# Distance attention: row normalisation, projections, norms and the first unit's stacks in one block

## The chip, the cores and the metric

The kernel runs on one core of a Trainium2 chip. Five engines work side by side: TensorE (PE; its weight loads are PEld), VectorE (DVE), ScalarE (ACT), GpSimd (POOL) and SyncE (SP), which here only issues DMAs. Each runs its own instructions in order, and they wait for one another on semaphores. The metric is the device time of one execution in microseconds, lower is better. The kernel before took 3648.4 us in the median of 3 runs (3647.82 to 3649.07).

## The reference

A "macaron" of six layers over `x` of 4 x 1024 x 128 in float32: a gelu feed-forward, a distance attention, the same feed-forward, two local-attention layers, a causal attention, and the two local layers again. Only the distance attention is changed. Its reference, where the input is the layer-normalised `x` and the result is added to `x`:

```python
Q = (x @ W_k.T).reshape(B, S, H, dk).transpose(0, 2, 1, 3)      # B=4, S=1024, H=16, dk=8
sq_norm = jnp.sum(Q * Q, axis=-1, keepdims=True)
dot = jnp.einsum('bhsk,bhtk->bhst', Q, Q)
scores = -(sq_norm - 2.0 * dot + sq_norm.transpose(0, 1, 3, 2)) * inv_sqrt_dk
attn = jax.nn.softmax(scores, axis=-1)
context_q = jnp.einsum('bhst,bhtk->bhsk', attn, Q)
merged = jnp.einsum('hkd,hvd->hkv', Wq_h, Wv_h)
attn_out = jnp.einsum('bhsk,hkv->bhsv', context_q, merged) * inv_sqrt_dk
return attn_out.transpose(0, 2, 1, 3).reshape(B, S, D) @ W_o.T
```

## The kernel before

The kernel is a sequence of blocks (`nc.Block()`). All engines meet at the end of a block, and `clear()` behind it is one more meeting of all engines that resets the semaphores. The stages of `distance_attention` are such blocks, in this order. `P` is 128, `NT` 32 tiles of 128 rows, `TPB` 8 tiles per batch.

1. A block in which SyncE issues the loads of the weights (L297 to L301).
2. `normalised_columns` (called in L302). It begins with `row_statistics`, one block (a table load and a square root on ScalarE, a reciprocal on VectorE). Then comes a block of eight steps of four tiles: VectorE normalises four rows of `xn` (`normalise`, L90, from SBUF to SBUF), TensorE transposes them into PSUM (L1319), ScalarE copies them to `xT` (L1330). `xn` has two buffers.
3. The projection block (L303 to L393). GpSimd sets `v`, `query` and `keys` with ten memsets of 128x1024 and then two small ones (L307 to L313). For each of 4 batches TensorE makes `q` in rows (L335, eight products, to slot 0) and in columns (L342, two products, to slot 1), and, one batch late, the squared norms (L327, to slot 2). ScalarE copies `q_all` (L361), then the high part `q_hi` (L364, rounded to float32r) and the squares `sq` (L367), then the high part of the norms `n_hl` (L356). VectorE subtracts to get the low parts: `q_lo` (L391) and the low half of `n_hl` (L384). All these VectorE operations have PSUM as a source. `merged` and `w_eff` are two 128x128 products of weights at the start.
4. The attention loop. A unit is one batch and four heads; there are 16. For each unit SyncE issues 40 DMAs from SBUF to SBUF (`stack`, L435 to L439) that lay the high and low parts of `q` and the norms one under the other in `query[k]` and `keys[k]`, k being 0 for even and 1 for odd units: 4 heads x 8 DMAs of 8 rows by 1024, and 2 of norms. The stack of unit u waits until unit u - 2 has made all its scores; those of units 0 and 1 wait for nothing. TensorE waits for the unit's 40 DMAs, then makes 32 jobs of scores (L466), ScalarE takes the exponential of each (L530, 128x1024), TensorE multiplies it with `v` (L481). Units 0 to 3 and 12 to 15 are written out; 4 to 11 are a hardware loop of two turns.
5. A block for the output product and the sum with `X` (L571, L578, L595).

What orders the work is only the order of the instructions on each engine and the semaphores.

Of the kernel before, what the change touches and what calls it, by code (L numbers as in the profile page):

```python
# [229 lines left out]
def distance_attention(nc, c, wk_d, wv_d, wo_d, sel_d):  # L230
# [17 lines left out]
    with ExitStack() as st:  # L248
# [16 lines left out]

        with ExitStack() as st2:
            sem, clear = semaphores(nc, st2, first=150)
            loaded = sem("loaded")
            q_ready = sem("q_ready")
# [14 lines left out]
            def sb2(name, shape, dt=F32):  # L284
                return st2.enter_context(nc.sbuf_tensor(c.fresh(name), shape, dt))
            xT = sb2("xT", [P, NT * P])
            wv = sb2("wv", [P, P])
# [14 lines left out]
            normalised_columns(nc, c, xT, moments=False)  # L302
            with nc.Block() as block:  # L303
                @block.gpsimd
                def _(pool):
                    for k in range(2):
                        pool.memset(v[k][:], 0.0).then_inc(cleared, 1)  # L307
                        for p in range(2):
                            pool.memset(query[k][p][:].bitcast(F32), 1.0).then_inc(cleared, 1)
                            pool.memset(keys[k][p][:].bitcast(F32), 1.0).then_inc(cleared, 1)  # L310
                    pool.wait_ge(cleared, 10)
# [4 lines left out]
                def _(pe):  # L316
                    pe.wait_ge(loaded, 80)
                    pe.matmul(c.slots[2][:, 0, 0:P], wv[:], wk[:], start=True, stop=True).then_inc(cross_ready, 1)

                    def norms(b):  # L320

                        pe.wait_ge(sq_ready, b + 1)
                        if b:
                            pe.wait_ge(norm_hi_ready, b)
                            pe.wait_ge(norm_lo_ready, b)
                        for half in range(2):
# [3 lines left out]

                    for b in range(B):
                        if b:
                            pe.wait_ge(q_out, b)
                        for t in range(TPB):
                            m = pe.matmul(c.slots[0][:, t // 4, (t % 4) * P:(t % 4 + 1) * P],  # L335
                                          xT[:, (b * TPB + t) * P:(b * TPB + t + 1) * P], wk[:], start=True, stop=True)
                        m.then_inc(q_ready, 1)
# [7 lines left out]
                        if b == 0:  # L345
                            pe.wait_ge(merged_ready, 1)
                            pe.matmul(c.slots[3][:, 0, 0:P], merged[:], wo[:], start=True, stop=True).then_inc(eff_ready, 1)
                        if b:
                            norms(b - 1)
                    norms(B - 1)  # L350

                @block.scalar
                def _(act):
                    def norm_out(b):
                        act.wait_ge(norm_ready, b + 1)
                        act.activation(n_hl[0:HEADS, b * S:(b + 1) * S], c.slots[2][0:HEADS].rearrange(flat),  # L356
                                       ACT.Copy).then_inc(norm_hi_ready, 1)

                    for b in range(B):
                        act.wait_ge(q_ready, b + 1)  # L360
                        act.activation(q_all[:, b * TPB:(b + 1) * TPB, :, :].rearrange("p t h d -> p (t h d)"),  # L361
# [6 lines left out]
                        if b:  # L368
                            norm_out(b - 1)
# [1558 lines left out]
```

## Time and profile before

| | |
|---|---|
| runs, median of 3 | 3648.4 us (3647.82 to 3649.07) |
| profiled execution | 3644.16 us |
| its span in the trace | 3642.4 us |
| TensorE's mean granted clock | 0.965 |
| PE busy | 3169.9 us, 87% of the span |
| VectorE busy | 2107.0 us, 58% |
| ScalarE busy | 2088.0 us, 57% |
| GpSimd busy | 1727.0 us, 47% |

The table is a mean over six layers with different limits. The page's list of 40 slices of the span shows the distance attention as the first long stretch without VectorE (its digit is 0 in slices 3 to 7, of 91 us each) and with TensorE at 9; ahead of it the second slice has TensorE at 5 only. For a single stage one reads the timeline and the waits of its own stretch; the times there count from the start of the span.

### The profile page before, as it was taken

The page shows a single profiled execution, that of the slowest core. Times are in us where ns is not written, and L with a number is a line of the kernel's source. Part 1 is how long each engine was busy: PE and PEld are TensorE (multiplying, and loading weights), DVE is VectorE, ACT ScalarE, POOL GpSimd, SP SyncE. Part 2 cuts the span into 40 slices and gives each one's busy share as a digit, 9 for nine tenths or more (in the row PEclk, how much of TensorE's full clock was granted, in tenths as well). Part 3 has the DMA queues.
Part 4 walks back from the last instruction along what each step waited for, and adds up shares of the span by engine and source line. Part 5 has one row for each costly group of instructions (what it writes and reads, how often), then busy time and mean ns, then how long its engine had stood idle before and what let it go on. Part 6 is the DMA issues. An engine that isn't in the chain of part 4 may idle for free. (4 is left out here: it accounts for less than half of the span.)

```text
span 3642.4 us, 72895 instructions
## 1 busy us (share of the span) xinstructions
PE 3169.9 (87%) x26438; PEld 1944.9 (53%) x26564; DVE 2107.0 (58%) x4204; ACT 2088.0 (57%) x3388; POOL 1727.0 (47%) x1348
## 2 busy tenths in 40 slices
PE   6599999858889988749999999999996688999885
PEld 4222222535566656526666666666664455666663
DVE  4200000458887777555555555555555688777773
ACT  2499999425555555435555555555553455555552
POOL 1100000058888888513333333333332788888882
PEclk9799999979999999979999999999998899999998
DMA  1122221021111111000000000000000211111111
GB/s 33 21 38 39 36 39 30 7 81 34 33 34 34 35 35 34 22 10 9 6 9 6 9 6 9 6 9 6 7 7 29 63 36 33 35 36 36 35 32 32
DMA packets 124405, 95.70 MB, mean 26 GB/s; under 512 B 80448, under 2 KB 100544, under 8 KB 123968
## 3 DMA queue, kind: packets, MB, share of 16 engines
q1 hardware_dynamic: 122784, 89.41, 11.2%
q10 hardware_dynamic: 1440, 3.80, 0.3%
q8 instruction: 122, 2.00, 0.2%
q14 instruction: 59, 0.48, 0.0%
HBM read 22.90 MB, written 2.10 MB: 7 GB/s over the span
## 5 line engine op out<-in xcount | busy, mean ns | idle before, releaser
L1737 POOL TENSOR_SCALAR e<-e,inv 128x768 f32<-128x768 f32 (+7 forms) x512 | 375.1, 745 | 763.6 <-DVE inv L1629 763.6
L1700 ACT ACTIVATE e<-e,nmax 128x768 f32<-128x768 f32 (+7 forms) x512 | 395.4, 772 | 429.6 <-DVE e L1624 427.1
L1624 DVE TENSOR_SCALAR_CACHE_REDUCE e<-slot 128x768 f32<-128x768 f32 (+7 forms) x512 | 376.5, 754 | 242.6 <-PE slot L1513 242.6
L530 ACT ACTIVATE e<-slot 128x1024 f32<-128x1024 f32 x512 | 472.5, 1087 | 38.0 <-PE slot L466 38.0
L880 POOL TENSOR_TENSOR inv_norm<-floored,minus_half 128x16 f32<-128x16 f32 x128 | 374.1, 2923 | 10.7
L1617 DVE COPY eT<-slot 128x512 f32<-128x512 f32 (+3 forms) x384 | 239.0, 622 | 235.4 <-PE slot L1524 235.3
L1117 ACT ACTIVATE probT<-slot 128x1024 f32<-128x1024 f32 x128 | 131.1, 1024 | 376.4 <-PE slot L973 376.4
L1524 PE MATMUL slot<-ident,e 128*128 128x128 f32 x2304 | 332.9, 280 | 8.4 <-DVE eT L1617 3.5
L852 POOL TENSOR_TENSOR prob<-prob,inv_total 128x1024 f32<-128x1024 f32 x128 | 242.7, 1896 | 200.4 <-DVE inv_total L1209 200.4
L1507 PE MATMUL slot<-key,q 64*128 64x512 f32 (+3 forms) x1536 | 318.1, 518 | 19.2 <-ACT v L1687 12.8
L873 POOL TENSOR_TENSOR rot<-cosine,sine 128x1024 f32<-128x1024 f32 x128 | 301.9, 2359 | 53.3 <-DVE sine L1191 53.2
L1524 PEld LDWEIGHTS slot<-ident,e 128*128 128x128 f32 x2304 | 253.2, 141 | 92.4 <-issue 69.4
L929 PE MATMUL slot<-w_qk,hT 128*128 128x512 f32 x512 | 259.2, 629 | 30.3 <-DMA b<-in_local_b_dram 18.7
L481 PE MATMUL slot<-e,v 128*32 128x512 f32 x2048 | 277.0, 614 | 0.4 <-ACT e L530 0.4
L1539 PE MATMUL slot<-eT,v 128*64 128x256 f32 x2048 | 254.6, 385 | 0.9 <-DVE X L1640 0.9
L466 PE MATMUL slot<-query,keys 36*128 36x512 f32 x1024 | 209.5, 474 | 45.3 <-DMA keys<-n_hl 31.8
L845 POOL TENSOR_TENSOR rot<-rot,inv_norm 128x1024 f32<-128x1024 f32 x128 | 243.5, 1902 | 0.3
L541 DVE COPY oT<-slot 128x512 f32<-128x512 f32 x32 | 22.1, 692 | 366.1 <-PE slot L481 366.1
L466 PEld LDWEIGHTS slot<-query,keys 36*128 36x128 f32 x1024 | 87.7, 187 | 267.9 <-ACT e L530 217.6
L449 POOL COPY v<-q_all 128x256 f32<-128x256 f32 (+1 forms) x16 | 6.4, 401 | 472.3 <-PE slot L481 449.8
L1094 ACT ACTIVATE sq<-slot 128x1024 f32<-128x1024 f32 x128 | 131.2, 1025 | 148.7 <-PE slot L929 148.7
L988 PE MATMUL slot<-probT,v_mix 128*64 128x64 f32 x2048 | 132.7, 228 | 88.5 <-ACT probT L1117 88.5
(158 smaller groups left out, 6443.7 us busy)
## 6 DMA issues: line engine op xcount, KB each, us to landing
v_mix<-v SPq DMA_DIRECT2D x256, 128.0 KB, 2.3
w_qkv<-in_causal_w_dram SPq DMA_DIRECT2D x32, 192.0 KB
query<-q_hi SPq DMA_DIRECT2D x128, 32.0 KB
keys<-q_hi SPq DMA_DIRECT2D x128, 32.0 KB
query<-q_lo SPq DMA_DIRECT2D x128, 32.0 KB
keys<-q_lo SPq DMA_DIRECT2D x128, 32.0 KB
hs<-H SPq DMA_DIRECT2D x32, 128.0 KB
h1s<-H SPq DMA_DIRECT2D x32, 128.0 KB
```

The source lines that it names most:

```text
L466: m = pe.matmul(out[:, h, :], keys[k][p][rows, t * P:(t + 1) * P], query[k][p][rows, half * 512:half * 512 + 512], start=True, stop=True)
L481: m = pe.matmul(c.slots[3][32 * j:32 * j + 32, half, :], v[k][:, t, j, :], e[(n - 1 + j // 2) % E_RING][:, j % 2 * 512:j % 2 * 512 + 512], ...
L530: act.activation(e[n % E_RING][:], c.slots[n % RING][:].rearrange(flat), ACT.Exp, scale=2 * SCALE).then_inc(e_ready, 1)
L873: pool.tensor_tensor(rot[:, a.j, :, :].rearrange(flat), cosine[:], sine[:], ALU.add).then_inc(rot_ready, 1)
L880: pool.tensor_tensor(inv_norm[:], floored[:], minus_half[:].broadcast_to([P, 2 * HEADS]), ALU.pow)\
L929: m = pe.matmul(bank_qk[:, half, :], hT[:, a.j * P:(a.j + 1) * P], w_qk[a.depth][:, half * 512:half * 512 + 512], start=True, stop=True)
L1507: pe.matmul(c.slots[h][:, bank, 0:hi - lo], q[k][rows, i * P:(i + 1) * P], key[k][rows, lo:hi], start=True, stop=True)
L1524: m = pe.transpose(turn[:, bank, t * P:(t + 1) * P], e[n % RING][h][:, (at + t) * P:(at + t + 1) * P], c.ident[:])
L1539: m = pe.matmul(o[64 * h:64 * h + 64, place(one) // 4, place(one) % 4 * P:(place(one) % 4 + 2) * P], v[k][:, t, 64 * h:64 * h + 64], eT[pa ...
L1624: dve.tensor_scalar(e[n % RING][h][:, 0:cols], c.slots[h][:].rearrange(flat)[:, 0:cols], -1.0, None, ALU.mult, ALU.min, accum_out=nmax[:, ...
L1700: act.activation(part, part, ACT.Exp, bias=nmax[:, n, h:h + 1], scale=-1.0, accum_out=total[:, n, h:h + 1]).then_inc(e_ready, 1)
L1737: pool.tensor_scalar(part, part, inv[:, n, h:h + 1], 1.0, ALU.mult, ALU.mult).then_inc(scaled, 1)
```

## The change

The normalisation of rows, their transposition, the projections and the norms become one block, and the DMAs of unit 0 are issued in it.

- Only `row_statistics` stays a block of its own. The rest of `normalised_columns` moves into the projection block; one block and one `clear()` go. The transposes now go to slot 3, and the small product for `w_eff` to slot 2.
- Per batch: TensorE makes columns, the transposes of the next batch's two groups, rows, norms. ScalarE: `q_hi`, `sq`, two copies of transposed columns, high norms, `q_all`. VectorE: eight rows of the next batch, `q_lo`, low norms. The norms are no longer one batch late.
- SyncE has a part in this block. It waits for five memsets and `q_hi` of batch 0, issues the 16 DMAs of the high parts, waits for `q_lo`, issues 16, waits for both parts of the norms, issues 8. GpSimd's memsets are reordered so that the buffers of even units and `v[0]` are the first five.
- In the loop, unit 0 has no stack left; unit 1 and the others keep theirs, with the same number of DMAs in another order within a head.
- The two `stacked` semaphores are made outside and cleared at the very end (`clear_stacked()`), one more meeting of all engines.

The functions `high`, `low` and `norms` of `stack_head` issue 4, 4 and 2 DMAs of a head. The diff, shortened:

```diff
+        def stack_head(sp, stacked, b, g, j):
+            k, cols = g % 2, bass.ds(b * S, S)
...
+            def high():
+                hi = q_hi[D * head:D * head + D, cols].bitcast(F32)
+                for at, dst in ((0, q_to), (0, k_to), (2, q_to), (1, k_to)):
+                    sp.dma_start(dst[to + at * D:to + at * D + D, :].bitcast(F32), hi).then_inc(stacked[k], 16)
+
+            def low():
+                lo = q_lo[D * head:D * head + D, cols].bitcast(F32)
+                for at, dst in ((1, q_to), (2, k_to), (3, q_to), (3, k_to)):
+                    sp.dma_start(dst[to + at * D:to + at * D + D, :].bitcast(F32), lo).then_inc(stacked[k], 16)
+
+            def norms():
+                both = n_hl[head:head + 33:32, cols].bitcast(F32)
+                sp.dma_start(q_to[to + 32:to + 34, :].bitcast(F32), both).then_inc(stacked[k], 16)
+                sp.dma_start(k_to[to + 34:to + 36, :].bitcast(F32), both).then_inc(stacked[k], 16)
+            return high, low, norms
+
+        stack_sem, clear_stacked = semaphores(nc, st, first=190)
+        stacked = [stack_sem("stacked_even"), stack_sem("stacked_odd")]
...
-            normalised_columns(nc, c, xT, moments=False)
+            row_statistics(nc, c, moments=False)
             with nc.Block() as block:
+                @block.sync
+                def _(sp):
+                    heads = [stack_head(sp, stacked, 0, 0, j) for j in range(GROUP)]
+                    sp.wait_ge(cleared, 5)
+                    sp.wait_ge(hi_ready, 1)
+                    for high, _, _ in heads:
+                        high()
+                    sp.wait_ge(lo_ready, 1)
+                    for _, low, _ in heads:
+                        low()
+                    sp.wait_ge(norm_hi_ready, 1)
+                    sp.wait_ge(norm_lo_ready, 1)
+                    for _, _, norms in heads:
+                        norms()
+
                 @block.gpsimd
                 def _(pool):
                     for k in range(2):
-                        pool.memset(v[k][:], 0.0).then_inc(cleared, 1)
                         for p in range(2):
                             pool.memset(query[k][p][:].bitcast(F32), 1.0).then_inc(cleared, 1)
                             pool.memset(keys[k][p][:].bitcast(F32), 1.0).then_inc(cleared, 1)
+                        pool.memset(v[k][:], 0.0).then_inc(cleared, 1)
                     pool.wait_ge(cleared, 10)
                     for k in range(2):
                         pool.memset(v[k][:, :, :, D:D + 1], 1.0).then_inc(cleared, 1)
 
...
+                    def turn_rows(i):
+                        pe.wait_ge(xn_ready, G * (i + 1))
+                        if i >= 2:
+                            pe.wait_ge(columns_ready, i - 1)
+                        for j in range(G):
+                            m = pe.transpose(c.slots[3][:, i % 2, j * P:(j + 1) * P], xn[:, i % 2, j, :], c.ident[:])
+                        m.then_inc(turned, 1)
+
+                    def columns(b):
+                        pe.wait_ge(columns_ready, 2 * b + 2)
                         if b:
                             pe.wait_ge(sq_ready, b)
                             pe.wait_ge(lo_ready, b)
...
+                    def rows(b):
+                        if b:
+                            pe.wait_ge(q_out, b)
...
+
+                    def norms(b):
+
+                        pe.wait_ge(sq_ready, b + 1)
+                        if b:
+                            pe.wait_ge(norm_hi_ready, b)
+                            pe.wait_ge(norm_lo_ready, b)
+                        else:
                             pe.wait_ge(merged_ready, 1)
-                            pe.matmul(c.slots[3][:, 0, 0:P], merged[:], wo[:], start=True, stop=True).then_inc(eff_ready, 1)
-                        if b:
-                            norms(b - 1)
-                    norms(B - 1)
+                            pe.wait_ge(eff_out, 1)
...
+                    pe.wait_ge(loaded, 80)
+                    pe.matmul(c.slots[2][:, 0, 0:P], wv[:], wk[:], start=True, stop=True).then_inc(cross_ready, 1)
+                    turn_rows(0)
+                    turn_rows(1)
+                    pe.wait_ge(merged_ready, 1)
+                    pe.matmul(c.slots[2][:, 1, 0:P], merged[:], wo[:], start=True, stop=True).then_inc(eff_ready, 1)
+                    for b in range(B):
+                        columns(b)
+                        if b < B - 1:
+                            turn_rows(2 * b + 2)
+                            turn_rows(2 * b + 3)
+                        rows(b)
+                        norms(b)
...
+                    def columns(i):
+                        act.wait_ge(turned, i + 1)
+                        act.activation(xT[:, i * G * P:(i + 1) * G * P], c.slots[3][:, i % 2, :], ACT.Copy).then_inc(columns_ready, 1)
+
+                    columns(0)
+                    columns(1)
                     for b in range(B):
...
                         act.wait_ge(qT_ready, b + 1)
                         act.activation(q_hi[:, b * S:(b + 1) * S], c.slots[1][:].rearrange(flat), ACT.Copy).then_inc(hi_ready, 1)
                         if b >= 2:
                             act.wait_ge(norm_ready, b - 1)
                         act.activation(sq[b % 2][:], c.slots[1][:].rearrange(flat), ACT.Square).then_inc(sq_ready, 1)
-                        if b:
-                            norm_out(b - 1)
-                    norm_out(B - 1)
+                        if b < B - 1:
+                            columns(2 * b + 2)
+                            columns(2 * b + 3)
+                        act.wait_ge(norm_ready, b + 1)
+                        act.activation(n_hl[0:HEADS, b * S:(b + 1) * S], c.slots[2][0:HEADS].rearrange(flat),
+                                       ACT.Copy).then_inc(norm_hi_ready, 1)
+                        act.wait_ge(q_ready, b + 1)
+                        act.activation(q_all[:, b * TPB:(b + 1) * TPB, :, :].rearrange("p t h d -> p (t h d)"),
+                                       c.slots[0][:].rearrange(flat), ACT.Copy).then_inc(q_out, 1)
...
                 def _(dve):
+                    def rows(i):
+                        if i >= 2:
+                            dve.wait_ge(turned, i - 1)
+                        for j in range(G):
+                            normalise(dve, c, i * G + j, xn[:, i % 2, j, :]).then_inc(xn_ready, 1)
+
+                    rows(0)
+                    rows(1)
                     dve.wait_ge(cross_ready, 1)
                     dve.wait_ge(loaded, 80)
                     dve.scalar_tensor_tensor(merged[:], c.slots[2][:, 0, 0:P], SCALE, block_mask[:], ALU.mult, ALU.mult)\
                        .then_inc(merged_ready, 1)
                     dve.wait_ge(eff_ready, 1)
-                    dve.tensor_copy(wo_eff[:], c.slots[3][:, 0, 0:P]).then_inc(eff_out, 1)
-
...
                     for b in range(B):
                         cols = slice(b * S, (b + 1) * S)
+                        if b < B - 1:
+                            rows(2 * b + 2)
+                            rows(2 * b + 3)
                         dve.wait_ge(hi_ready, b + 1)
                         dve.wait_ge(sq_ready, b + 1)
                         dve.tensor_tensor(q_lo[:, cols], c.slots[1][:].rearrange(flat), q_hi[:, cols].bitcast(F32),
                                           ALU.subtract).then_inc(lo_ready, 1)
-                        if b:
-                            norm_low(b - 1)
-                    norm_low(B - 1)
+                        dve.wait_ge(norm_hi_ready, b + 1)
+                        dve.tensor_tensor(n_hl[32:32 + HEADS, cols], c.slots[2][0:HEADS].rearrange(flat),
+                                          n_hl[0:HEADS, cols].bitcast(F32), ALU.subtract).then_inc(norm_lo_ready, 1)
             clear()
...
                     def stack(b, g, first=False, last=False):
-                        k, cols = g % 2, bass.ds(b * S, S)
-                        if not first and not (isinstance(b, int) and b == 0 and g == 1):
+                        if first:
+                            return
+                        if not (isinstance(b, int) and b == 0 and g == 1):
                             sp.wait_ge(s_ready, JOBS * (GROUPS * b + g - 1))
...
+                            for part in stack_head(sp, stacked, b, g, j):
+                                part()
...
             clear()
+        clear_stacked()
```

## Rows read from the trace of the kernel before

**Rows 1.** Waits from 160 to 660 us (total, times, longest).
```profile
ACT e L530 <- PE slot L466: 38.0, 22, 28.3
...
PE slot L466 <- DMA keys<-n_hl: 31.8, 1, 31.8
```

**Rows 2.** Timeline from 137 us: start, duration, engine, line; idle time in brackets.
```profile
137.85 0.89 SPq L435 DMA_DIRECT2D query<-q_hi  x1
137.86 1.28 ACT L524 ACT_TABLE_LOAD   x1 [2.00 <-PEq L38]
...
164.77 0.51 SPq L439 DMA_DIRECT2D keys<-n_hl  x1
...
166.58 1.65 PE L466 MATMUL slot<-query,keys 36*128 36x512 f32 x6 [31.78 <-DMA keys<-n_hl]
...
167.42 5.61 ACT L530 ACTIVATE e<-slot 128x1024 f32<-128x1024 f32 x6 [28.28 <-PE slot L466]
```

**Rows 3.** Timeline, the normalised columns.
```profile
95.25 2.14 DVE L90 TENSOR_SCALAR xn<-X,moments,rstd 128x128 f32<-128x128 f32 x8 [0.73 <-PEq L38]
...
96.42 2.14 PE L1319 MATMUL slot<-ident,xn 128*128 128x128 f32 x8 [10.80 <-DVE xn L90]
...
97.57 0.60 ACT L1330 ACTIVATE xT<-slot 128x512 f32<-128x512 f32 x1 [3.44 <-PE slot L1319]
```

**Rows 4.** Timeline, the projection block.
```profile
106.12 0.95 POOL L307 MEMSET v<- 128x1024 f32 x1 [25.68 <-SPq L303]
...
108.24 1.88 PE L342 MATMUL slot<-xT,wk 128*128 128x512 f32 x4
...
110.16 1.02 ACT L364 ACTIVATE q_hi<-slot 128x1024 fp32r<-128x1024 f32 x1 [0.69 <-PE slot L342]
...
115.16 0.21 POOL L313 MEMSET v<- 128x32 f32 x2
...
120.98 1.89 PE L327 MATMUL slot<-sq,sel 128*16 128x512 f32 x4
...
131.27 3.53 PE L327 MATMUL slot<-sq,sel 128*16 128x512 f32 x4 [2.87 <-DVE n_hl L384]
...
135.88 1.21 DVE L384 TENSOR_TENSOR n_hl<-slot,n_hl 16x1024 fp32r<-16x1024 f32 x1 [4.76 <-ACT n_hl L356]
```

**Rows 5.** Timeline of SyncE's issues, stack of unit 2 and first issue of unit 3.
```profile
196.28 0.68 SPq L435 DMA_DIRECT2D query<-q_hi  x1
...
223.16 0.51 SPq L439 DMA_DIRECT2D keys<-n_hl  x1
...
225.96 0.68 SPq L435 DMA_DIRECT2D query<-q_hi  x1
```

**Rows 6.** Timeline of short windows, VectorE's rows beside GpSimd (local layers).
```profile
747.99 1.21 DVE L1174 TENSOR_SCALAR H<-X,moments,rstd 128x128 f32<-128x128 f32 x1 [1.10 <-PEq L38]
...
748.35 0.30 POOL L900 MEMSET kT<- 128x256 f32 x1
...
748.60 0.51 POOL L901 MEMSET v_mix<- 64x512 f32 x1
...
906.14 1.90 POOL L852 TENSOR_TENSOR prob<-prob,inv_total 128x1024 f32<-128x1024 f32 x1 [2.56 <-DVE inv_total L1209]
906.17 1.95 DVE L1174 TENSOR_SCALAR H<-X,moments,rstd  x1 [0.20 <-issue]
...
2807.62 1.59 DVE L1174 TENSOR_SCALAR H<-X,moments,rstd 128x128 f32<-128x128 f32 x1 [0.73 <-PEq L38]
```

**Rows 7.** Windows: stretch, length, busy PE, PEld, DVE, ACT, POOL, PE clock, DMA.
```profile
96.00:100.00 4.00, 3.40 (x13) 2.39 (x14) 3.63 (x15) 1.30 (x3) 0.00 (x0) 0.50 0.00 0
...
100.50:105.00 4.50, 2.90 (x18) 1.69 (x16) 3.60 (x15) 2.54 (x5) 0.00 (x0) 1.00 0.00 0
...
128.00:131.00 3.00, 0.40 (x1) 0.00 (x0) 2.32 (x2) 1.45 (x2) 0.00 (x0) 1.00 0.00 0
...
408.00:417.00 9.00, 9.00 (x40) 2.10 (x36) 0.69 (x1) 5.82 (x6) 0.40 (x1) 0.50 0.29 44
```

More of the change, by code:

```diff
@@ L263, in distance_attention @@
         ctx_all = sb("ctx_all", [P, NT, P])
+        def stack_head(sp, stacked, b, g, j):
+            k, cols = g % 2, bass.ds(b * S, S)
+            head = GROUP * g + j
+            to, q_to, k_to = 64 * (j % 2), query[k][j // 2], keys[k][j // 2]
+            def high():
[13 more added lines that the diff above has]
+        stacked = [stack_sem("stacked_even"), stack_sem("stacked_odd")]
         with ExitStack() as st2:
@@ L316, in _ @@
                 def _(pe):
[L317 to L322, printed above, removed]
-                        if b:
-                            pe.wait_ge(norm_hi_ready, b)
-                            pe.wait_ge(norm_lo_ready, b)
-                        for half in range(2):
-                            m = pe.matmul(c.slots[2][0:HEADS, half, :], sel[:], sq[b % 2][:, half * 512:half * 512 + 512],
-                                          start=True, stop=True)
-                        m.then_inc(norm_ready, 1)
-                    for b in range(B):
-                        if b:
[L333 to L337, printed above, removed]
+                    def turn_rows(i):
[7 more added lines that the diff above has]
+                        pe.wait_ge(columns_ready, 2 * b + 2)
                         if b:
@@ L344, in _ @@
                         m.then_inc(qT_ready, 1)
-                        if b == 0:
-                            pe.wait_ge(merged_ready, 1)
-                            pe.matmul(c.slots[3][:, 0, 0:P], merged[:], wo[:], start=True, stop=True).then_inc(eff_ready, 1)
-                        if b:
-                            norms(b - 1)
-                    norms(B - 1)
+                    def rows(b):
+                        if b:
+                            pe.wait_ge(q_out, b)
+                        for t in range(TPB):
+                            m = pe.matmul(c.slots[0][:, t // 4, (t % 4) * P:(t % 4 + 1) * P],
+                                          xT[:, (b * TPB + t) * P:(b * TPB + t + 1) * P], wk[:], start=True, stop=True)
+                        m.then_inc(q_ready, 1)
@@ new lines, in norms @@
+                    def norms(b):
[4 more added lines that the diff above has]
+                        else:
+                            pe.wait_ge(merged_ready, 1)
+                            pe.wait_ge(eff_out, 1)
+                        for half in range(2):
+                            m = pe.matmul(c.slots[2][0:HEADS, half, :], sel[:], sq[b % 2][:, half * 512:half * 512 + 512],
+                                          start=True, stop=True)
+                        m.then_inc(norm_ready, 1)
```

32 lines of the change are left out of this document (7 added, 25 removed).

## Prediction

> **What bounds the kernel now.** I read the list of waits first, between the start and the end of the attention loop. It shows one long wait of TensorE there, 31.8 us for a DMA into `keys`, once; ScalarE's exponentials waited 28.3 us for the same reason [rows 1]. Inside the loop ScalarE runs one exponential of 128x1024 after the other and nothing else ends late. So the loop itself is not touched by this change, and what can be won lies before its first score. The timeline of that stretch has three parts. The stacks: SyncE issues the 40 DMAs of unit 0 from 137.85 to 165.28, one after the other, and the first score matmul starts at 166.58, 1.3 us after the last issue [rows 2]. Before them, the normalised columns: VectorE's rows start at 95.25 and pass through TensorE and ScalarE [rows 3], until the next block opens at 106.1. Between the two, the projections: from 106.1 on; the last norm ends at 137.09, and the next block starts 0.76 us later [rows 2, 4]. Every stage waits for the end of the one before it, so 95.25 to 166.58, 71.3 us, is one chain. The question is how long it is when the three lie in one block.
>
> **The stacks.** All 40 DMAs are still issued, in another order (16 of the high parts, 16 low, 8 norms), so their issue takes the same 27.4 us [rows 2]. They now start when `hi_ready` of batch 0 and five memsets are there. They leave the path as long as the projections last longer than 27.4 us from that point on; below that is so by 2.5 us, and if that cover is lost SyncE ends the block and each microsecond counts in full. Queued behind SyncE's three waits is nothing but these DMAs. Unit 1's stacks move too: before, they were issued straight behind unit 0's, a little before the first score; now they start with the new loop block, with the first score. That is the position that all later units have: 40 issues from 196.28 to 223.67, plus the 1.3 us to land, against 29.68 us from one unit to the next [rows 5]. That fits with about 1 us to spare; I take nothing for it, between 0 and 1 us of loss.
>
> **The first batch of the merged block.** Let R be the start of VectorE's first row. Eight rows take 2.14 us [rows 3]; 0.1 to TensorE; the second four transposes at the low clock 1.1 (eight in 2.14) [rows 3]; the copy with its two hand-overs 0.8 (0.60 of it the copy) [rows 3]. Then `columns(0)`, four passes of 128x512, 1.88 at the full clock [rows 4]; the same count of passes at the low clock took 3.53 [rows 4]; as the clock rises in this stretch I take 2.7. Then the next two groups of transposes 1.1, `rows(0)` 1.95 (eight products, estimated from the 1.9 of its neighbours) [rows 4], `norms(0)` 1.89 [rows 4]. Norms of batch 0 are out at R + 11.8.
>
> **The period of the batches.** The old block needed 5.5 us a batch. The new one is slower, because VectorE now has the rows of the next batch queued behind `norm_low`: norms out of TensorE; high part on ScalarE 1.0, low part on VectorE 1.21 [rows 4], two groups of rows 2.14 [rows 3], one group of transposes 0.55 after the last, `rows` 1.95, `norms` 1.89, hand-overs 0.2: 8.95 us. Meanwhile TensorE has only `columns` to do, so it idles about 1.7 us in each. Two such periods are 17.9 us. The last batch has no rows: ScalarE is busy 2.0 us with the high norms and `q_all` of batch 2, then copy and square to 3.95, norms to 6.0, their two halves to 8.25. From R to the last low norm: 11.8 + 17.9 + 8.25 = 37.95 us.
>
> **What the change puts beside VectorE's rows.** The ten GpSimd memsets of `v`, `query` and `keys` stood in the projection block, where VectorE read PSUM. Now they start with the rows. They are back to back: 0.95 us each, and 9.04 us from the first to the two small ones behind them [rows 4]. What a row of this very form does beside GpSimd is in the trace: a row of 128x128, 0.26 us when alone, began at 747.99 in the middle of a string of memsets and took 1.21, ending when the 0.51 us memset of `v_mix` ended; the boundaries of several shorter memsets passed without it. The same in the second layer stage: 2807.62, until after the same memset [rows 6]. Beside a single tensor_tensor of GpSimd the row lasted 1.95 us, until that one ended, and passed before the next [rows 6]. GpSimd's first instruction comes out of a barrier about as early as VectorE's (both within 0.2 us), so one row may slip ahead, not eight. The cost of the ten memsets is thus bounded by 0 (no blocking) and 9.0 us (the rows wait for the whole string). I take 9.0, as the nearest rows are strings of memsets, and several boundaries passed there without the row. The Trainium skill (SBUF — State Buffer, "Who interferes with whom") says that VectorE in its two-port mode and GpSimd share a port pair as an exclusive lock, and that the later one blocks until the earlier instruction finishes. By that rule one row would pass at every boundary; rows 6 agree for tensor_tensor and differ for the short memsets. That result is the first rival below.
>
> **The sum.** R is 95.25 now and 95.2 + 9.0 = 104.2 after. Last low norm 104.2 + 37.95 = 142.15; block change 0.76 as now; first score 143.0 instead of 166.58: 23.6 us earlier. Off that go 0.35, since the exponential table load of 1.28 us, now hidden under the stacks [rows 2], starts with the first score, which needs 0.84 to the first exponential; and 0.4 for the extra barrier of `clear_stacked` (between 0 and the 0.76 of a whole block change). GpSimd's first `v` copy (first used five jobs later) costs nothing. Net 22.8 us. `hi_ready` comes at about R + 7.9 = 112.1, SyncE is done at 139.6, 2.5 us before the projections. Profiled: 3642.4 - 22.8, span 3619.6. The profiled execution took 3644.16, the runs 3648.4 in the median; I subtract from the median: 3625.6, rounded to 3625.
>
> **Rivals.**
> *One row passes at each memset boundary.* Eight rows then need about eight memsets, 7.2 us plus their own time, and the second group ends near 103.3 instead of 106.3. It saves 2.8 more: 3622.5. For it: the tensor_tensor case and that these memsets are long; against it: the missed boundaries [rows 6].
> *No blocking.* R stays 95.25, 9.0 us better: 3616.5. It would hold if memsets of this size never exclude a row; nothing in rows 6 supports that, except that the products that VectorE reads from PSUM ran beside the memsets unchanged.
> *TensorE stays at 1.2 GHz in the merged block.* The clock fell at 131 after a stretch with 0.40 us of matmuls in 3.0 [rows 7]; the new idle 1.7 us per batch is shorter, but broken up by transposes only. Price: transposes, `rows` and `norms` double, some 4.2 us in each of three batches and 5 in the last: 3625 + 17 = 3642. The Trainium skill (TensorE: Matmul & The Clock Gate, "Part 4: PE-mode transpose") says that transposes do not count as activity for the full clock, which would favour this. The trace contradicts it: transposes alone ran from 96.4, and the granted clock was 0.50 until 100 and 1.00 from 100.5 [rows 7].
> *The change does not hide the stacks.* If issues beside the busy block take over 2.5 us longer in all, SyncE ends the block: 3626 to 3630.
> *Slower than before.* The loop starts after a shorter pause, and if the clock did not rise for it, a job would cost 1.5 us (6 jobs in 9.0 us at the low clock) [rows 7] instead of 29.68 / 32 = 0.93. At 0.57 us a job the gain of 22.8 is gone after 40 jobs beyond those that start slowly now. Nothing points there: TensorE's pause before the loop shrinks from 31.8 us to about 3.
> Small either way: the loop's start may find the clock high (1.5 us better), and one low stretch at 408 [rows 7] may fall away or come twice, 3.4 us (the 3.4 jobs lost in 9 us).
>
> **Chances.** Whole string blocks 0.43 (3622 to 3629), one row per boundary 0.26 (3619 to 3626), no blocking 0.18 (3613 to 3619), low clock 0.05, stacks not hidden 0.05, slower 0.03. To leave out no more than 2 in 10 the range must reach most of the no-blocking case: 3615 to 3630. Faster by over 0.2% (7.3 us, about what a measurement can tell from no change) is all but the last case and most of the low clock: 0.95; within it 0.03; slower 0.02.
>
> **What would show it.** First row of `xn` several microseconds long and ending with a memset; ten memsets back to back from 95.2; first `q_hi` copy near 111; first stack issue right behind it, the last near 139; the norms of successive batches 9 us apart; first score at 143, with no wait for a DMA. Rows of 0.34 us beside memsets mean no blocking and 3616. Norms 13 us apart mean the low clock. A PE wait for `keys` at the second unit means unit 1's stacks are late. The stages from 500 us on should only be shifted.

## Result, and the profile after

The changed kernel took 3617.3 us in the median of 4 runs (3614.5 to 3625.4), the kernel before 3648.1 (4 runs): ratio 0.9919, 95% interval 0.9902 to 0.9936, faster by 0.8%. The trace kept is that of its longest run, 3625.43 us, with a span of 3623.6; a second series of the same kernel (e8 below) had 3618.1 and a trace with a span of 3615.0.

The timeline of the changed kernel from its first row to the first scores (start, duration, engine, line, idle time in brackets; lines are those of the changed kernel, L90 the rows, L366 the transposes, L425 `q_hi`, L397 the norms, L465 the low norms, L274 the stacks, L529 the scores):

```profile
95.04 0.95 POOL L352 MEMSET query<- 128x1024 f32 x1 [14.66 <-POOLq L38]
...
95.09 4.16 DVE L90 TENSOR_SCALAR xn<-X,moments,rstd 128x128 f32<-128x128 f32 x8 [0.73 <-PEq L38]
95.94 1.09 POOL L353 MEMSET keys<- 128x1024 f32 x1
...
101.09 4.08 DVE L90 TENSOR_SCALAR xn<-X,moments,rstd 128x128 f32<-128x128 f32 x8
...
104.37 1.02 ACT L425 ACTIVATE q_hi<-slot 128x1024 fp32r<-128x1024 f32 x1 [3.31 <-PE slot L375]
...
105.48 0.89 SPq L274 DMA_DIRECT2D query<-q_hi  x1
...
107.61 1.89 PE L397 MATMUL slot<-sq,sel 128*16 128x512 f32 x4
...
111.82 2.14 DVE L90 TENSOR_SCALAR xn<-X,moments,rstd 128x128 f32<-128x128 f32 x8
...
117.94 1.89 PE L397 MATMUL slot<-sq,sel 128*16 128x512 f32 x4
...
126.73 1.89 PE L397 MATMUL slot<-sq,sel 128*16 128x512 f32 x4
...
131.72 0.50 SPq L284 DMA_DIRECT2D keys<-n_hl  x1
...
135.58 1.22 DVE L465 TENSOR_TENSOR n_hl<-slot,n_hl 16x1024 fp32r<-16x1024 f32 x1 [1.74 <-ACT n_hl L433]
137.90 0.72 SPq L274 DMA_DIRECT2D query<-q_hi  x1
...
137.95 1.65 PE L529 MATMUL slot<-query,keys 36*128 36x512 f32 x6 [3.45 <-PEq L38]
...
139.21 5.60 ACT L593 ACTIVATE e<-slot 128x1024 f32<-128x1024 f32 x6
```

Read against [rows 2 to 4]: the loop block opens at 137.90, where it opened at 137.85 before. The merged block is not shorter than the two that it replaces. What is gone is the stretch between the opening of the loop block and the first score: 28.7 us before (137.85 to 166.58), next to nothing now (137.90 to 137.95). The stacks are issued inside the block, from 105.48 to 132.2, and the score no longer waits for a DMA (its releaser is the block's start).

The first score comes 28.6 us earlier (166.58 before, 137.95 now). Of these, 18.8 are left in the span of this trace. The exponentials start 0.42 later behind the score (1.26 against 0.84). From the first to the last of the 512 exponentials the loop took 487.0 us against 481.1, and the rest of the kernel behind it 2997.4 against 2993.8: 28.6 - 0.4 - 5.9 - 3.6 = 18.7. The 5.9 lie almost all at the start of the loop, where the first 20 exponentials took 25.4 us against 19.8. These are windows of that start: first those of this trace, then those of the same kernel in e8, last those of the kernel before (stretch, length, busy PE, PEld, DVE, ACT, POOL, granted clock, DMA).

```profile
138.00:161.60 23.60, 22.67 (x88) 6.07 (x92) 0.00 (x0) 17.48 (x19) 0.67 (x2) 0.50 0.27 41
162.00:180.00 18.00, 17.24 (x124) 5.18 (x124) 1.93 (x4) 17.57 (x20) 0.41 (x1) 1.00 0.16 23
```

```profile
136.40:145.50 9.10, 8.16 (x32) 2.65 (x32) 0.00 (x0) 8.36 (x9) 0.74 (x2) 0.50 0.26 38
145.70:170.00 24.30, 23.55 (x164) 6.96 (x160) 1.24 (x3) 23.82 (x27) 0.00 (x0) 1.00 0.25 38
```

```profile
167.00:175.00 8.00, 7.50 (x32) 2.18 (x30) 0.00 (x0) 6.86 (x8) 0.00 (x0) 0.50 0.29 43
176.00:200.00 24.00, 23.25 (x162) 6.83 (x160) 1.24 (x3) 23.67 (x26) 0.00 (x0) 1.00 0.23 35
```

The clock stood at 1.2 GHz for 23.6 us of the loop here, with TensorE busy 22.7 of them, for 9.1 us in e8, and for about 9 us before the change (from 166.58 to between 175 and 176). At that clock a job takes about 1.5 us and at full clock 0.93.

### The profile page after: what moved, and what is told of

Read it like the earlier page. It is cut to its first block and busy times, and to the rows that moved or that the text cites. A ratio compares the mean times of both kernels' runs of the same rounds, so it can differ in the third digit from the quotient of the medians.

```text
span 3623.6 us, 73013 instructions
## 1 busy us (share of the span) xinstructions
PE 3204.1 (88%) x26564; PEld 1949.2 (54%) x26564; DVE 2110.4 (58%) x4204; ACT 2088.5 (58%) x3388; POOL 1730.5 (48%) x1348
## 5 line engine op out<-in xcount | busy, mean ns | idle before, releaser
L1181 ACT ACTIVATE probT<-slot 128x1024 f32<-128x1024 f32 x128 | 131.1, 1024 | 374.9 <-PE slot L1037 374.9
L1571 PE MATMUL slot<-key,q 64*128 64x512 f32 (+3 forms) x1536 | 318.5, 519 | 19.1 <-ACT v L1751 12.8
L529 PE MATMUL slot<-query,keys 36*128 36x512 f32 x1024 | 210.9, 477 | 17.7 <-ACT e L593 11.3
L529 PEld LDWEIGHTS slot<-query,keys 36*128 36x128 f32 x1024 | 88.5, 189 | 241.5 <-ACT e L593 219.6
L1052 PE MATMUL slot<-probT,v_mix 128*64 128x64 f32 x2048 | 133.3, 229 | 88.8 <-ACT probT L1181 88.8
```

Source lines behind the costliest of these rows:

```text
L529: m = pe.matmul(out[:, h, :], keys[k][p][rows, t * P:(t + 1) * P], query[k][p][rows, half * 512:half * 512 + 512], start=True, stop=True)
L1571: pe.matmul(c.slots[h][:, bank, 0:hi - lo], q[k][rows, i * P:(i + 1) * P], key[k][rows, lo:hi], start=True, stop=True)
```

## Experiments

All traces in one table. "Score - row" is the time from VectorE's first row to the first score, which takes out how early the stage began; "20 exp." is the time from the first to the 21st exponential. The ratios are to the kernel before on the same chip.

| | first row | first `q_hi` | last low norm ends | first score | score - row | 20 exp. | median us | ratio, 95% |
|---|---|---|---|---|---|---|---|---|
| before | 95.25 | 110.16 | 137.10 | 166.58 | 71.3 | 19.8 | 3648.1 | |
| changed | 95.09 | 104.37 | 136.79 | 137.95 | 42.9 | 25.4 | 3617.3 | 0.9919 (0.9902 to 0.9936) |
| e8, changed again | 93.47 | 102.31 | 135.26 | 136.41 | 42.9 | 19.6 | 3618.1 | 0.9925 (0.9908 to 0.9941) |
| e1, stacks only | 95.08 | 111.63 | 137.42 | 141.23 | 46.2 | 25.3 | 3623.7 | 0.9932 (0.9915 to 0.9950) |
| e2, merge only | 95.31 | 105.15 | 135.72 | 165.57 | 70.3 | 19.5 | 3648.6 | 1.0000 (0.9990 to 1.0009) |
| e3, memsets early | 97.67 | 105.01 | 138.43 | 139.58 | 41.9 | 19.6 | 3616.4 | 0.9911 (0.9894 to 0.9927) |
| e4, warm start | 94.35 | 103.42 | 136.12 | 137.73 | 43.4 | 19.6 | 3618.4 | 0.9919 (0.9903 to 0.9936) |
| e5, rows later | 94.17 | 103.61 | 134.09 | 135.25 | 41.1 | 19.9 | 3616.2 (one run) | |
| e6, rows first | 94.65 | 103.72 | 130.03 | 133.29 | 38.6 | 24.2 | 3615.6 | 0.9916 (0.9899 to 0.9932) |
| e7, both | 93.91 | 101.37 | 126.78 | 131.04 | 37.1 | 23.0 | 3613.9 | 0.9909 (0.9893 to 0.9926) |
| e9, e7 warm | 94.41 | 100.97 | 126.38 | 130.62 | 36.2 | 25.3 | 3615.1 | 0.9917 (0.9900 to 0.9933) |
| e11, GpSimd issues a head | 93.86 | 101.24 | 126.64 | 127.61 | 33.8 | 22.9 | 3607.3 | 0.9901 (0.9885 to 0.9918) |

The runs of one kernel on one chip lie within 2 to 13 us of one another (the kernel before: 3641.8 to 3654.8 over all chips), and each interval but that of e2 reaches some 6 us to either side, so the times do not tell the changed versions from one another. The positions in the traces separate them better, but they are one trace for each version and two for the changed kernel.

### e1: the stacks without the merge

```diff
             normalised_columns(nc, c, xT, moments=False)
             with nc.Block() as block:
+                @block.sync
+                def _(sp):
+                    heads = [stack_head(sp, stacked, 0, 0, j) for j in range(GROUP)]
+                    sp.wait_ge(cleared, 5)
+                    sp.wait_ge(hi_ready, 1)
...
```

> The kernel before, with the change's SyncE part in its old projection block (and its order of memsets); rows, transposes and projections stay in two blocks. Theory A (nearly all the gain is the stacks, the merging only brings the first high part forward): the first q_hi is at 111.2 as before, SyncE issues for 27.4 us and is done at 138.7, 1.6 us after the last norm, so SyncE now ends the block; first score near 139.8, 26.8 us earlier than before and about 2 us later than in the changed kernel; time 3648 - 26 = 3622, or up to 5 us more if the clock at the loop's start stays low as long as in the changed kernel. Rival B (the gain needs the merged block, since SyncE's issues slow down or are slowed beside the projections): first score at 145 or later.

The timeline at the end of its block (L422 the low norms, L284 the last stacks):

```profile
136.21 1.21 DVE L422 TENSOR_TENSOR n_hl<-slot,n_hl 16x1024 fp32r<-16x1024 f32 x1 [3.62 <-ACT n_hl L394]
...
139.42 0.51 SPq L284 DMA_DIRECT2D keys<-n_hl  x1
141.15 0.68 SPq L274 DMA_DIRECT2D query<-q_hi  x1
...
141.23 1.22 PE L496 MATMUL slot<-query,keys 36*128 36x512 f32 x4 [6.10 <-DMA keys<-n_hl]
```

First score at 141.2, 25.4 us earlier than before: 1.4 later than I expected, far from the 145 of B. SyncE ends the block here, 2.5 us behind the last norm. A holds: the stacks alone give 25.2 of the 28.5 us that the whole change gives between first row and first score (71.3 to 46.2, to 42.9). The ratio, 0.9932, is 0.1% above the changed kernel's, inside both intervals.

### e2: the merge without the stacks

```diff
-                @block.sync
-                def _(sp):
-                    heads = [stack_head(sp, stacked, 0, 0, j) for j in range(GROUP)]
...
-                        if first:
-                            return
-                        if not (isinstance(b, int) and b == 0 and g == 1):
+                        if not first and not (isinstance(b, int) and b == 0 and g == 1):
```

> The changed kernel with unit 0's stacks back in the loop block; the merged block stays. Theory A: the merged block ends where the two old ones ended (137.8 against 137.85 in the traces), so the first score is at 166.6 as before and the time is that of before plus the extra barrier of 0.4 us: 3648 to 3649. Rival B (the merging gains on its own by the barrier and block that it removes, 0.7 us and more): 3640 or less, first score at 160.

```profile
134.51 1.21 DVE L450 TENSOR_TENSOR n_hl<-slot,n_hl 16x1024 fp32r<-16x1024 f32 x1 [1.75 <-ACT n_hl L418]
136.86 0.88 SPq L274 DMA_DIRECT2D query<-q_hi  x1
...
165.57 0.80 PE L512 MATMUL slot<-query,keys 36*128 36x512 f32 x2 [32.15 <-DMA keys<-n_hl]
```

The old wait for the DMA is back, 32.15 us. Score - row is 70.3 against 71.3; the ratio is 1.0000 with an interval of 0.1% on both sides. A holds. From the first row to the first score the merge alone gives 1 us where its periods run at the full clock (8.8, 8.8 and 5.9 us between the norms of its batches). In the changed kernel's own trace, which had one low stretch of the clock, it gives nothing: 42.8 us from the first row to the opening of the loop block, against 42.6 before. With the stacks inside it is worth 3.3 us (e1 to changed), since it brings the first `q_hi` and with it SyncE's start forward by 7.3 us (the first `q_hi` 16.6 us behind the first row in e1, 9.3 in the changed kernel).

### e3 and e5: the memsets beside the rows

e3 moves the memsets into the block that loads `x`; e5 has the rows ask in the middle of a memset.

```diff
# e3, in the block that loads x; query, keys and v are allocated ahead of it
+            @block.gpsimd
+            def _(pool):
+                for k in range(2):
+                    for p in range(2):
+                        pool.memset(c.query[k][p][:].bitcast(F32), 1.0).then_inc(cleared, 1)
...
# e5
+                    for t in range(2):
+                        dve.bn_stats(c.stats[:, t, :], c.X[:, t, :])
                     rows(0)
                     rows(1)
```

> The changed kernel with the ten memsets (and the two small ones) moved to the block that loads x, where VectorE takes only statistics; the buffers live longer. Theory A (each pair of rows waited for one memset in the merged block: 8 rows took 4.16 and 4.08 us instead of 2.14): rows take 2.14 both times, hi_ready comes 3 to 4 us earlier, the last norm and the first score 4 us earlier than in the changed kernel (near 134), and the load block is not longer as it waits for its DMAs. Rival B (the rows are slow because of something else, the semaphores or the cold start): 8 rows still take 4 us, first score at 138. In time A gives 3613 against 3617, with several us of scatter from the clock.

> The changed kernel with two spare statistics instructions (about 0.5 us, one SBUF source, result unused) ahead of VectorE's first rows, so that the first row asks in the middle of a memset and not 0.04 us after its start. In the memset string of the load block of e3 a cast asked 0.44 us into a memset and passed only when the string had ended, 4.1 us later, over four boundaries; in the changed kernel two rows passed at each boundary. Theory A (it depends on when the row asks): the first rows wait for several memsets or the whole string, up to 9 us, first q_hi at 110 or later. Rival B (rows pass at every boundary whenever they ask; the cast was held for another reason): two rows per memset as before, first q_hi within 1 us of the changed kernel's 104.4 (its stage starting at the same time).

In e3 both sets of eight rows took 2.14 and 2.13 us, so the memsets had been the cause of the 4.16 and 4.08 of the changed kernel: theory A. The first `q_hi` came 7.3 us after the first row, against 9.3. The first score followed the first row by 41.9 us, only 1.0 earlier, because this trace has two low stretches of the clock in the block (its batches were 10.4, 10.4 and 5.9 us apart). And the load block got longer. VectorE's two casts, 0.23 and 0.22 us in the changed kernel, took 4.14 and 4.07 there, beside the memsets:

```profile
5.18 0.95 POOL L1852 MEMSET query<- 128x1024 f32 x1
5.63 4.14 DVE L1874 CAST ident_bf<-ident 128x128 bf16<-128x128 f32 x1 [4.75 <-DMA future<-in_const_causal_dram]
5.77 4.07 DVE L1875 CAST causal<-future 128x128 bf16<-128x128 f32 x1
6.07 0.95 POOL L1853 MEMSET keys<- 128x1024 f32 x1
6.96 0.95 POOL L1852 MEMSET query<- 128x1024 f32 x1
7.85 0.95 POOL L1853 MEMSET keys<- 128x1024 f32 x1
8.73 0.95 POOL L1854 MEMSET v<- 128x1024 f32 x1
9.75 0.23 POOL L1857 MEMSET v<- 128x32 f32 x2
```

The first ended at 9.77, with the string: four boundaries passed without it, as in [rows 6]. In the merged block the rows did pass. Short windows of the changed kernel (the first row ended at 96.07, and the next memset, 0.95 alone, took 1.09), and below of e5:

```profile
95.04 0.95 POOL L352 MEMSET query<- 128x1024 f32 x1 [14.66 <-POOLq L38]
...
95.09 0.98 DVE L90 TENSOR_SCALAR xn<-X,moments,rstd 128x128 f32<-128x128 f32 x1 [0.73 <-PEq L38]
```

```profile
93.73 0.95 POOL L352 MEMSET query<- 128x1024 f32 x1 [13.14 <-POOLq L38]
...
93.98 0.28 DVE L448 BATCH_NORM_STATS2 stats<-X 128x6 f32<-128x128 f32 x1
94.17 0.59 DVE L90 TENSOR_SCALAR xn<-X,moments,rstd 128x128 f32<-128x128 f32 x1
```

In e5 the first row asked 0.44 us into the memset, as the cast of e3 had (0.45), and was out at 94.76, 0.08 us after the memset's end; eight rows took 3.76 us. The statistics ahead of it ran inside the memset in 0.28 us. So in this one trace the moment of asking did not decide, and theory A of e5 falls. In all six traces of merged blocks with memsets two rows passed at each boundary. Why the cast, and the rows at 747.99 and 2807.62, had to wait for several boundaries stays open.

### e6 and e7: the chain of the periods

```diff
# e6
...
-                        if b < B - 1:
-                            rows(2 * b + 2)
-                            rows(2 * b + 3)
+                        if b == 0:
+                            rows(2)
+                            rows(3)
                         dve.wait_ge(hi_ready, b + 1)
...
                                           ALU.subtract).then_inc(lo_ready, 1)
+                        if b < B - 2:
+                            rows(2 * b + 4)
+                            rows(2 * b + 5)
                         dve.wait_ge(norm_hi_ready, b + 1)
...
# e7: e6 and the memsets of e3, five of them held back
...
+                    if k == 0:
+                        pool.wait_ge(constants_ready, 3)
```

> The changed kernel with VectorE's rows of batch b+2 ahead of its low norms of batch b instead of behind them. Theory A (the period of the merged block is set by the chain norms, high norms, low norms, rows, transposes; 8.8 us at the full clock, 10.3 with a low stretch): the period falls to TensorE's own work, about 7 us, the last low norm comes near 131, SyncE's last issue stays at 132.2 and now ends the block: first score near 133.8, 4 us earlier than the changed kernel. Rival B (the period is set by TensorE and the clock): first score within 1 us of 138. Time under A 3613, with several us of scatter.

> e6 with the memsets in the block that loads x: five before its constants arrive, five behind the two casts of VectorE, so that neither the casts (which waited 4.1 us in e3) nor the rows meet them. Theory A (memsets cost 4 us beside the rows and SyncE's start follows the first q_hi): first q_hi near 100.5, SyncE done near 128.5, first score near 130.4, about 7.5 us earlier than in the changed kernel, time near 3610. Rival B (the load block gets longer by as much, as in e3, where all stages behind it came 2.5 to 3.9 us later): the stage starts later and the first score is no earlier than in e6.

In e6 the norms of the batches are 6.4, 6.4 and 5.9 us apart. The last low norm was out at 130.0, but the first score only at 133.3:

```profile
128.81 1.21 DVE L468 TENSOR_TENSOR n_hl<-slot,n_hl 16x1024 fp32r<-16x1024 f32 x1 [1.74 <-ACT n_hl L433]
...
131.07 0.50 SPq L284 DMA_DIRECT2D keys<-n_hl  x1
133.25 0.72 SPq L274 DMA_DIRECT2D query<-q_hi  x1
...
133.29 1.65 PE L532 MATMUL slot<-query,keys 36*128 36x512 f32 x6 [5.56 <-PEq L38]
```

Theory A of both: the period of 8.8 us was the chain through the rows behind the low norms, and once it is cut, SyncE ends the block. In e7 the load block was no longer than before (first row at 93.91), `q_hi` came 7.5 us behind the first row, and the first score at 131.0, 0.6 later than expected. The next block opened 1.2 us after SyncE's last issue in e1, 1.7 in e6 and 1.8 in e7, against 1.1 after the last low norm in the changed kernel. The expectations of e6 and e7 had 1.6 and 1.9 from there to the first score, that of e1 1.1; why it differs stays open. The medians, 3615.6 and 3613.9, are 1.7 to 4.2 us below the changed kernel's two (3617.3 and 3618.1), less than the traces show (4.3 and 5.8 us from first row to first score) and within the scatter.

### e4, e8 and e9: the start of the loop

```diff
# e4 (3 products) and e9 (6, on top of e7)
                         rows(b)
                         norms(b)
+                    for k in range(3):
+                        pe.matmul(c.slots[3][:, k % 2, :], wk[:], xT[:, 0:512], start=True, stop=True)
```

> The changed kernel with three spare products of 128x512 on TensorE (into slot 3, read by nobody) behind the last norms, where TensorE idles 3.4 us before the loop: some 2.6 us of matmuls. Theory A (5.2 us of the gain were given back at the loop's start since the granted clock was 0.50 from 137.8 to 161.7, 23.9 us, where it was low for 9 us of the old loop): the clock stays at 1.00 across the start of the loop, the first 20 exponentials come at 0.92 us each, and the time is 5 to 6 us below the changed kernel's slow executions, near 3612, with less scatter. Rival B (the start of the loop is slow because of its DMAs of unit 1, which now run beside it from the first job): the clock is high and the first 20 jobs are still slow; time unchanged at 3617.

> The changed kernel once more, to see a second trace of it. Theory A (the start of the loop has two paces, by how long the granted clock stays at 1.2 GHz there, and which it takes changes from execution to execution): the first score is at 137.9 within 2 us as in the first trace, and the 20th exponential comes 19.6 us behind the first (as in the traces of before, e2, e3, e4) or 25.4 us (as in the changed kernel and e1); its times scatter over some 8 us. Rival B (the change makes the start of the loop slow each time, for instance by unit 1's DMAs beside it): 25.4 us again in any trace of it.

> e7 with six spare products of 128x512 on TensorE behind the last norms (5.2 us at the full clock, while SyncE's last DMAs still keep the block open). In e4 the clock was 1.00 when the loop began and fell 2.3 us later for 6.8 us, and the first 20 jobs took the shorter of the two times seen. Theory A (what TensorE does in the 6 us ahead of the loop decides how long the start is slow): the first 20 exponentials take 18.5 to 19.6 us instead of the 22.95 of e7, time 3 us below e7, near 3611. Rival B (the first jobs themselves, with idle time between them and 36 rows in use, let the clock fall or stay low whatever came before; how long is chance): the clock falls within 4 us of the first score, 20 exponentials take anything from 19.6 to 25.4, and the median is e7's within 2 us.

e8 has the same code as the changed kernel, and 20 exponentials took 19.6 us, not 25.4. So the slow start is not made by the change each time, nor by unit 1's DMAs beside it: theory A of e8, and my rival there falls. Over the twelve traces the same 20 jobs took 19.5 to 19.9 us in six and 22.9 to 25.4 in six. The latter are the changed kernel's first trace and those of e1, e6, e7, e9 and e11, with one trace each, so that some versions start slowly more often than others is neither shown nor excluded. The spare products of e4 came with a short start (19.6), yet the median was 3618.4, no better. With those of e9 the start was slow:

```profile
125.00:130.50 5.50, 4.43 (x11) 1.69 (x9) 1.21 (x1) 1.04 (x2) 0.00 (x0) 1.00 0.07 16
131.00:133.60 2.60, 1.09 (x8) 0.34 (x4) 0.00 (x0) 2.59 (x3) 0.34 (x2) 1.00 0.27 39
133.80:154.00 20.20, 20.00 (x80) 4.97 (x84) 0.00 (x0) 14.10 (x16) 0.00 (x0) 0.50 0.28 42
```

The clock was at 2.4 GHz when the loop began (130.62); TensorE, which waits for exponentials there, was busy 1.09 of the 2.6 us from 131.0 on; the clock fell to 1.2 GHz and stayed there for 20 us with TensorE busy throughout. Rival B of e9: full-size products right ahead of the loop do not keep the clock up in it. How long the first jobs stay at 1.2 GHz is not explained by any of these runs.

### e11: GpSimd issues a quarter of the stack

```diff
# on top of e7
+                    heads = [stack_head(sp, stacked, 0, 0, j) for j in (0, 1, 2)]
...
+                @block.gpsimd
+                def _(pool):
+                    heads = [stack_head(pool, [stacked_pool], 0, 0, j) for j in (3,)]
...
```

> e7 with the ten DMAs of head 3 of unit 0 issued by GpSimd instead of SyncE (a semaphore of their own). Theory A (in e7 SyncE's 40 issues end the block: last issue done at 129.2, last low norm at 128.0 less 1.2, first score at 131.04): SyncE needs 30 issues, done near 122.5, and the first score follows the last low norm by 1.2 us as in the changed kernel: near 128.0, 3 us earlier than in e7. Rival B (GpSimd's issues are slower than SyncE's 0.65 us, 2.5 us or more each, and their DMAs land after the last norms): first score at 131 or later.

```profile
102.58 0.82 POOL L272 DMA_DIRECT2D query<-q_hi  x1 [21.89 <-ACT q_hi L425]
103.40 0.54 POOL L272 DMA_DIRECT2D keys<-q_hi  x1
...
121.94 0.50 SPq L282 DMA_DIRECT2D keys<-n_hl  x1
...
125.43 1.21 DVE L468 TENSOR_TENSOR n_hl<-slot,n_hl 16x1024 fp32r<-16x1024 f32 x1 [1.74 <-ACT n_hl L433]
127.41 0.68 SPq L272 DMA_DIRECT2D query<-q_hi  x1
...
127.61 1.40 PE L534 MATMUL slot<-query,keys 36*128 36x512 f32 x6 [3.26 <-PEq L38]
```

SyncE is done at 122.4, the last low norm at 126.6, and the first score comes at 127.6, 3.4 us earlier than in e7: theory A. GpSimd issued its DMAs in 0.52 to 0.58 us each behind a first one of 0.82, so B falls. This is the fastest version tried: 3607.3 us, ratio 0.9901 (0.9885 to 0.9918). Its runs (3604.9 to 3611.0) all lie below all eight runs of the changed kernel (3614.5 to 3625.4), but they come from another chip, on which the kernel before was faster too (3643.7), and the intervals of the ratios overlap. That it is faster is shown by its trace up to the first score, and not by the times.

## Why the prediction was right, point by point

The median lies in the range, 8 us below the forecast of 3625. The mechanism was right, and the number was helped by luck. By the prediction's own cases 3617.3 would belong to "no blocking" (3613 to 3619), and the rows were blocked: the range reached down to 3617.3 only because it took in most of a case that did not happen. With the measured terms in place of the forecast ones the sum gives 3620.6, and the rest, 3.3 us, is within what executions of the changed kernel differ by (3614.5 to 3625.4). The steps:

*What bounds the kernel.* Right. The wait of 31.8 us [rows 1] is gone, and nothing else in the loop took its place.

*The stacks.* Right: the issues took 26.7 us in the block (27.4 forecast), were not slowed by the work beside them, and were done 4.6 us before the last low norm (2.5 forecast). Unit 1's stacks made no one wait.

*The first batch, R + 11.8.* In e3, without memsets, the norms of batch 0 were out 11.8 us after the first row (97.67 to 109.45). Inside it two errors cancel: its first `q_hi` was ready 8.4 us after the first row and not 7.9.

*The period.* 8.8 us at the full clock (8.95 computed); the first in this trace took 10.3, because the clock was at 1.2 GHz from 113.9 to 117.3:

```profile
110.00:114.00 4.00, 2.06 (x8) 0.76 (x6) 3.39 (x10) 3.70 (x5) 0.00 (x0) 0.98 0.32 47
114.00:117.00 3.00, 2.98 (x14) 2.98 (x15) 1.09 (x1) 0.88 (x2) 0.00 (x0) 0.50 0.33 48
```

That is a single stretch of the rival in which the clock stays low for the whole block; its price was 1.5 us, not 17. The two periods were 19.1 us instead of 17.9. The last batch took 8.2 (8.25). What sets the period was right too: e6 takes the rows out of that chain, and it falls to 6.4.

*The memsets.* This is the term that was mis-sized. I took 9.0 us, the whole string. The rows were blocked, but two of them passed at each boundary, so the norms of batch 0 came 14.4 us after the first row instead of 11.8: 2.6 us, and 2.0 for the first `q_hi`. The other traces of merged blocks agree: with the memsets beside the rows they have 14.2 to 14.6 us here, and without them 11.8 to 11.9 (e3, e7, e11) and 11.0 (e9). The first rival had the right mechanism with one row instead of two per boundary. Rows of short memsets [rows 6] were the wrong neighbour for long ones, and the lock as the Trainium skill describes it (SBUF — State Buffer, "Who interferes with whom") gave the better number here; the casts of e3 show that neither covers all cases.

*The sum.* First score 143.0 forecast, 137.95 measured: -6.4 for the memsets, +1.2 for the low stretch, +0.3 for the block change (1.1, not 0.76), and -0.1 each for R and the last batch. Some small slips of the working change no case: 3625.6 rounds to 3626, the two ends of the first rival differ by 3.0 and not by 2.8, and the low stretch at 408 loses 3.4 us, which is 3.7 jobs. The table load cost 0.42 (0.35), and the extra barrier 0.40: from the last moments to the first load of the next layer 1.12 us instead of 0.72, exactly as taken.

*The loop's start.* I called it small, 1.5 us better. It was 5.9 us worse in the changed kernel's first trace and 0.3 better in its second. The rival "slower than before" had named this mechanism: ten more jobs at 1.5 us each, where forty would have been needed. That I saw nothing pointing there was an error: the kernel before, too, ran its first 9 us of the loop at 1.2 GHz, and nothing in its trace said that this would not get longer. Why it got longer in one trace and not in the other stays open.

*The rest.* The stages behind the loop took 2992.7 to 2997.8 us in the twelve traces, 2997.4 in the changed kernel and 2993.8 before. e1, with the same extra barrier, has 2993.9, and e8, the changed kernel again, 2996.5. The difference goes with the granted clock: of the eleven traces of changed versions, the five with 2996.5 to 2997.8 have 189 to 203 us of that stretch at 1.2 GHz, the six with 2992.7 to 2994.8 have 178 to 186. Whether the edit or the execution sets that is not shown.

## What to carry to other kernels

Look first for the queue that only issues: 40 small DMAs at 0.50 to 0.65 us were 27 us of waiting for everyone, and moving their start into the work before gave nearly all of the gain, while merging the compute stages gave 1 us by itself. Merging pays as far as it lets the issuing queue start earlier; after that the last of two chains counts, and a third engine that issues a part of the DMAs shortens it (e11). When an operation is moved beside another engine's, ask what it shares with it: ten hidden memsets cost 2.6 us once VectorE read and wrote SBUF beside them.

## What the runs showed of the hardware

- Back-to-back memsets of 128x1024 on GpSimd let two queued VectorE rows (SBUF to SBUF, float32) through at each boundary, and the memset behind them took 1.09 us instead of 0.95. Two queued casts from float32 to bfloat16 beside the same memsets did not pass at four boundaries and took 4.14 and 4.07 us. VectorE's statistics (one input in SBUF, 6 results a row) ran inside such a memset in 0.28 us.
- TensorE was busy with the loop's scores and values for 22.7 of 23.6 us, and the clock stayed at 1.2 GHz; in another execution of the same code it rose after 9.1 us. Full-size products ahead of the loop did not prevent the fall in e9.
- GpSimd issued DMAs between SBUF tensors of 8 rows by 1024 in 0.52 to 0.54 us each (the first in 0.82), SyncE in 0.65.
